# Fourteen scatter-add streams, clearing in 1.6 KB packets and a reordered update stage in a graph network kernel

## The chip, the cores and the metric

One core of a Trainium2 chip runs the whole program once. The metric is the device time of that run in microseconds (us). The times of the kernel before are 3835.6, 3843.22 and 3844.84 us; the median is 3843.22 us.

## What is computed

The input is a graph of 3,125 nodes and 50,000 edges, sorted by destination (`dst`), with 128 numbers a node. Four graph networks follow one another, each with a residual sum and a layer norm behind it:

```python
for l in range(2):                       # first network, a typed graph transformer
    k, q, v = (typed_linear(h, ntype, W) for W in (Wk[l], Wq[l], Wv[l]))
    kT, vT = k x Watt[l, head, etype], v x Wmsg[l, head, etype]   # for all 32 edge types
    att = edge_softmax((kT[src, etype] * q[dst]).sum() * pri / sqrt(16), dst)
    hag = segment_sum(vT[src, etype] * att, dst)
    h = silu(typed_linear(hag, ntype, Wa[l])) * alpha + h * (1 - alpha)
    h = (h - mean) * rsqrt(var + 1e-5) * g + b
# second network: sums over neighbours; third: radial network silu(silu(e8 @ A1 + b1) @ A2 + b2) @ A3
# on 8 edge features; fourth: two graph convolutions with batch norm
```

The second and the fourth network sum over neighbours by a product with a dense matrix of 3,200 x 3,200 counts (how many edges lead from node to node).

## The kernel before, in words

**Stages.** Each stage is a block of its own: all engines meet at its end. In order: `prepare` (indices), then for each of the two layers `project` (`qkv`), `relation_table` (`tab`), `attention` (`att`) and `update` (`upd`); then the other networks, where `adjacency` reads the count matrix three times.

**The count matrix** lies in HBM. Each of its rows has 3,200 cells and 8 more (`AW = NP + STREAMS`), one for the end of each stream. It is cleared by 25 DMAs of 1604 KB each (`wipe_matrix`, L433 to L436), which write a node's row of 12.8 KB as one packet; six of them are issued in `prepare`, nineteen in `project` of layer 0, on SP's queue, behind 16 small loads of marks (`load_chunks`). `query_rows`, 25.7 MB, is cleared in `prepare` in the same way by 16 DMAs (L240). `K.wiped` and `K.cleared` count them; only POOL waits for them, at the start of `tab0` (L1499).

**Scatter-adds.** The 50,176 edges are 392 tiles of 128. For each tile POOL issues one indirect DMA that adds 128 numbers to 128 cells (L1465), after `search` on VectorE has merged the repeats in a tile. The tiles form 8 streams of 49 consecutive tiles, and two tiles of one stream may meet in a cell; so the add number i of a stream waits until number i-1 has landed (`added[k]`). A turn is one tile of each stream. Fixed numbers of turns lie in the stages (`COUNTS`), in tiles: 112 in each `tab`, 24 in each `att`, 48 in each `upd`, 24 in `qkv1`. The search goes by units of the same eight tiles.

**`relation_table`.** TensorE makes keys and values for all 32 types, VectorE and ScalarE copy them from PSUM, SP stores them in 100 DMAs of 1 MB (L1524). Meanwhile POOL scatters 25 tiles of query rows (L1501), issues four gathers (L1506), and then its scatter-adds; a last direct DMA (L1511) and the wait for all landings end the stage on POOL.

**`update`.** n = 10 rounds of four slots. POOL gathers a round's attention sums (four DMAs, L718), from the third round on with four scatter-adds behind them, and issues the rest at the end. VectorE scales (`scale`), TensorE transposes (`flip`), ScalarE copies (`turn`), TensorE multiplies by the typed weight (L761), ScalarE applies silu (L815), VectorE blends with h and takes mean and variance (`blend`), ScalarE takes the root (L797), VectorE the reciprocal (`finish`), ScalarE normalises (L789), VectorE applies gain and shift (`grade`). Between a round's transposes and its typed products both engines do the round's radial pairs (two or three of 24 or 25 in all): two matmuls with 512 columns (L732, L739), two silus (L772, L779) and a store on ScalarE's queue (L781).

## Time and profile before

| what | value |
|---|---|
| time of the profiled execution | 3847.27 us |
| its span | 3845.6 us |
| median of three runs | 3843.22 us |
| busy: TensorE, VectorE, ScalarE, POOL | 68%, 47%, 29%, 57% of the span |
| mean granted TensorE clock | 0.776 of full speed |
| DMA, mean | 227 GB/s |
| the 392 scatter-adds (L1465) | 620.0 us busy, 1.58 us each, 255.1 us idle before them, of which 185.9 us behind the landing of an earlier one |
| `prepare` and `qkv0`, then `tab0` | to 306 us, to 625 us |
| `att0`, `upd0`, `qkv1`, `tab1` | to 1205, 1361, 1465, 1783 us |
| `att1`, `upd1` | to 2368, 2528 us |

"Busy" is the time in which an engine executes; an issue of an indirect DMA counts as work of POOL. Idle time is put down to what ended it. The page's chain of waits covers only the last microseconds of the program, so the stages have to be read one by one.

### The profile page before, as it was taken

The page shows a single profiled execution, that of the slowest core. Times are in us where ns is not written, and L with a number is a line of the kernel's source. Part 1 is how long each engine was busy: PE and PEld are TensorE (multiplying, and loading weights), DVE is VectorE, ACT ScalarE, POOL GpSimd, SP SyncE. Part 2 cuts the span into 40 slices and gives each one's busy share as a digit, 9 for nine tenths or more (in the row PEclk, how much of TensorE's full clock was granted, in tenths as well). Part 3 has the DMA queues.
Part 4 walks back from the last instruction along what each step waited for, and adds up shares of the span by engine and source line. Part 5 has one row for each costly group of instructions (what it writes and reads, how often), then busy time and mean ns, then how long its engine had stood idle before and what let it go on. Part 6 is the DMA issues. An engine that isn't in the chain of part 4 may idle for free. (4 is left out here: it accounts for less than half of the span.)

```text
span 3845.6 us, 42073 instructions
## 1 busy us (share of the span) xinstructions
PE 2610.9 (68%) x11696; PEld 1711.6 (45%) x11696; DVE 1813.0 (47%) x4239; ACT 1122.4 (29%) x2928; POOL 2202.2 (57%) x1985
## 2 busy tenths in 40 slices
PE   1537992666662658992666663638968888859696
PEld 1325662555551335662555552334444444434343
DVE  6524442555562455442555552431058888830303
ACT  0113440222221743440222222730034555510001
POOL 4316557777777876557777777860047777720000
PEclk9966555888876875555788786868969999969797
DMA  9988996898975448996898884447546666547372
GB/s 350 310 339 320 395 391 155 259 266 263 268 224 109 73 120 306 396 391 169 255 263 261 267 235 94 92 133 235 194 117 192 188 187 190 153 169 271 123 272 85
DMA packets 656434, 872.83 MB, mean 227 GB/s; under 512 B 120594, under 2 KB 540761, under 8 KB 615653
## 3 DMA queue, kind: packets, MB, share of 16 engines
q1 hardware_dynamic: 298564, 567.61, 42.0%
q0 software_dynamic: 120320, 158.13, 18.0%
q10 hardware_dynamic: 237360, 144.89, 12.3%
q8 instruction: 79, 1.29, 0.1%
q14 instruction: 111, 0.90, 0.1%
HBM read 441.21 MB, written 429.28 MB: 226 GB/s over the span
## 5 line engine op out<-in xcount | busy, mean ns | idle before, releaser
L1698 POOL DMA_INDIRECT att_rows<-table,kvrow x784 | 797.4, 1017 | 247.6 <-issue 232.8
L1465 POOL DMA_INDIRECT matrix<-count,place x392 | 620.0, 1582 | 255.1 <-DMA matrix<-count,place 185.9
L2101 POOL DMA_INDIRECT msg_rows<-rows,msg_src x392 | 404.0, 1031 | 338.1 <-DMA msg_src<-in_src_pt 218.9
L1756 PE MATMUL att_po<-att_message,att_mate 128*128 128x264 f32 (+1 forms) x1568 | 394.5, 407 | 10.8 <-ACT att_out L1824 5.4
L1548 DVE COPY tab_part<-tab_bank 128x512 f32<-128x512 f32 x400 | 257.5, 686 | 294.4 <-DMA table<-tab_part 276.3
L1589 PE MATMUL tab_bank<-wk,tab_kv 32*128 32x256 f32 x1600 | 363.9, 696 | 30.5 <-DVE tab_part L1548 19.2
L1725 PE MATMUL att_pq<-a,att_mate 128*128 128x128 f32 x1152 | 215.2, 347 | 223.3 <-DVE att_prod L1882 222.8
L1756 PEld LDWEIGHTS att_po<-att_message,att_mate 128*128 128x128 f32 x1568 | 305.9, 238 | 65.2 <-DVE att_message L1933 26.2
L1882 DVE TENSOR_TENSOR att_prod<-att_rows,att_pq 128x512 f32<-128x512 f32 x196 | 134.8, 688 | 424.0 <-DMA att_rows<-table,kvrow 423.6
L1589 PE MATMUL tab_bank<-wv,tab_kv 32*128 32x256 f32 x1600 | 332.2, 618 | 0.0
L1573 ACT ACTIVATE tab_part<-tab_bank 128x512 f32<-128x512 f32 x400 | 221.7, 594 | 312.8 <-DMA table<-tab_part 297.8
L1725 PEld LDWEIGHTS att_pq<-a,att_mate 128*128 128x128 f32 x1152 | 194.5, 252 | 252.8 <-issue 249.0
L1409 PE MATMUL gsum_acc<-gsum_cells,h_rows 128*128 128x512 f32 (+1 forms) x700 | 287.6, 563 | 17.0 <-DMA gsum_cells<-matrix 17.0
L1824 ACT ACTIVATE att_out<-att_po 128x136 f32<-128x136 f32 (+1 forms) x784 | 224.6, 336 | 243.4 <-PE att_po L1756 236.4
L1589 PEld LDWEIGHTS tab_bank<-wk,tab_kv 32*128 32x128 f32 x1600 | 204.4, 302 | 179.6 <-DVE tab_part L1548 149.1
L1589 PEld LDWEIGHTS tab_bank<-wv,tab_kv 32*128 32x128 f32 x1600 | 234.6, 321 | 12.4
L1725 PE MATMUL att_pq<-att_query,att_mate 128*128 128x128 f32 x416 | 78.8, 350 | 195.4 <-DMA att_query<-query_rows 103.6
L1409 PEld LDWEIGHTS gsum_acc<-gsum_cells,h_rows 128*128 128x128 f32 x700 | 131.2, 193 | 174.7 <-issue 157.2
L2155 ACT ACTIVATE msg_sc<-msg_rows,msg_edge 128x128 f32<-128x128 f32 x392 | 125.3, 390 | 264.9 <-DMA msg_rows<-rows,msg_src 261.5
L2139 PE MATMUL msg_pm<-msg_prod,down 128*128 128x512 f32 x392 | 189.4, 607 | 3.0 <-DVE msg_total L2228 1.4
L1874 DVE TENSOR_TENSOR att_mate<-att_rank,rank_own 128x512 f32<-128x512 uint8 x196 | 134.3, 685 | 97.7 <-DMA att_rank<-rank 97.7
L2112 PE MATMUL msg_pu<-ident,msg_sc 128*128 128x128 f32 x784 | 110.7, 284 | 102.3 <-ACT msg_un L2163 88.1
(403 smaller groups left out, 4147.2 us busy)
## 6 DMA issues: line engine op xcount, KB each, us to landing
table<-tab_part SPq DMA_DIRECT2D x200, 1024.0 KB
gsum_cells<-matrix SPq DMA_DIRECT2D x50, 1604.0 KB
att_sums<-att_out ACTq DMA_DIRECT2D x196, 272.0 KB
matrix<-a SPq DMA_DIRECT2D x25, 1604.0 KB
nb_cells<-matrix SPq DMA_DIRECT2D x25, 1604.0 KB
a<-query_rows SPq DMA_DIRECT2D x144, 256.0 KB
query_rows<-a SPq DMA_DIRECT2D x16, 1568.0 KB
att_message<-in_ea_rows SPq DMA_DIRECT2D x98, 256.0 KB, 4.6
```

Source lines behind the costliest of these rows:

```text
L1409: nc.tensor.matmul(acc[c][:, 0:m], rows[:, i, :], cells[i % R][:, part(c)], start=i == 0, stop=False)
L1465: nc.gpsimd.indirect_dma_start(D.matrix, bass.IndirectOffsetOnAxis(ap=K.place[:, col:col + 1], axis=0), K.count[:, col:col + 1], None, com ...
L1548: nc.vector.tensor_copy(quad_columns(c // 2, c % 2), bank[c // 2 % 2 * 4 + c % 2][:, :].rearrange("p (n r d) -> p n r d", n=2, d=QUAD)).th ...
L1573: nc.scalar.activation(quad_columns(c // 2, 2 + c % 2), bank[c // 2 % 2 * 4 + 2 + c % 2][:, :].rearrange("p (n r d) -> p n r d", n=2, d=QUAD),
L1589: last = nc.tensor.matmul(bank[q % 2 * 4 + quad][:, k * (W // 2):(k + 1) * (W // 2)], kv[u][rows, k, :], w[rows, q * 8:q * 8 + 8, :].rearr ...
L1698: nc.gpsimd.indirect_dma_start(rows[g % RR][:, j, :], None, D.table, bass.IndirectOffsetOnAxis(ap=K.kvrow[:, t:t + 1], axis=0)).then_inc(r ...
L1725: last = nc.tensor.matmul(pq[g % 2][:, j * P:(j + 1) * P], mate[g % RS][:, j, :], query[g % RQ][:, j, :], start=True, stop=True)
L1756: nc.tensor.matmul(po[j][:, 0:w], mate[h % RS][:, j, :], message[h % RM][:, j, 0:w], start=True, stop=True).then_inc(summed, 1)
L1824: nc.scalar.activation(out[k][:, j, 0:w], po[j][:, 0:w], ACT.Copy).then_inc(copied, 1)
L1882: nc.vector.tensor_tensor(prod[g % 2][:, :, :], rows[g % RR][:, :, 0:P], pq[g % 2][:, :].rearrange("p (j d) -> p j d", j=J), ALU.mult).the ...
L2101: nc.gpsimd.indirect_dma_start(rows[g % RR][:, j, :], None, D.rows, bass.IndirectOffsetOnAxis(ap=src[:, t:t + 1], axis=0)).then_inc(rows_i ...
L2139: nc.tensor.matmul(pm[n][:, :], down[n][:, :], prod[n][:, :], start=True, stop=True).then_inc(mapped, 1)
```

## The change

Three things are changed.

1. **Streams.** 14 streams of 28 tiles in place of 8 of 49. The adds are placed tile by tile (`count_part`) and no longer by whole turns: 140 in each `tab`, 24 in each `att`, 24 in each `upd`, 16 in `qkv1`. The search keeps its units of eight (`SEEK`). A matrix row grows from 3,208 to 3,216 cells.
2. **Clearing.** Both clearings write packets of 1.6 KB (1,568 B and 1,608 B) from one zero strip in place of 12.5 and 12.8 KB. Three wipes are in `prepare`, 22 in `project`, now ahead of the marks' loads.
3. **Update.** The roots, reciprocals and means of five rounds are taken at once, twice a stage; a round's typed products stand ahead of its radial pairs, and the transposes of round k+1 ahead of the products of round k, on TensorE and on ScalarE; the hidden rows are stored by SP in place of ScalarE; the next layer's weights are loaded behind the radial network's; POOL adds five tiles a round in rounds 4 to 8, and none in the first four.

```diff
-STREAMS = 8
+STREAMS = 14
...
+COUNTS = {"qkv0": range(0), "tab0": range(0, 140), "att0": range(140, 164), "upd0": range(164, 188),
+          "qkv1": range(188, 204), "tab1": range(204, 344), "att1": range(344, 368), "upd1": range(368, TILES)}
+UPDATE_TILES = 5
+AW = NP + 16
+STRIP = AW // 8
...
-EARLY_WIPES = 6
+EARLY_WIPES = 3
...
-                sp.dma_start(rows[:, i * WIPE:(i + 1) * WIPE], K.zero[:, 0:WIPE]).then_inc(K.cleared, 16)
+                sp.dma_start(rows[:, i * WIPE:(i + 1) * WIPE].rearrange("p (b c) -> p b c", b=8),
+                             K.zero[:, 0:WIPE // 8].unsqueeze(1).broadcast_to([P, 8, WIPE // 8])).then_inc(K.cleared, 16)
...
-        sp.dma_start(cells[i], K.zero[:, 0:AW]).then_inc(K.wiped, 16)
+        sp.dma_start(cells[i].rearrange("p (b c) -> p b c", c=STRIP),
+                     K.zero[:, 0:STRIP].unsqueeze(1).broadcast_to([P, AW // STRIP, STRIP])).then_inc(K.wiped, 16)
...
+def count_part(nc, K, D, pool, cols, added, begin, end):
+
+    for i in range(begin, min(end, len(cols))):
+        k = cols[i] % STREAMS
+        if i >= STREAMS:
+            pool.wait_ge(added[k], i // STREAMS * 16)
+        nc.gpsimd.indirect_dma_start(D.matrix, bass.IndirectOffsetOnAxis(ap=K.place[:, cols[i]:cols[i] + 1], axis=0),
+                                     K.count[:, cols[i]:cols[i] + 1], None, compute_op=ALU.add).then_inc(added[k], 16)
```

The update's orders, TensorE and ScalarE, and VectorE below:

```diff
+            flip_in(0)
+            for k in range(n):
+                kinds = [nc.tensor.value_load(K.tile_type[0:1, k * J + j:k * J + j + 1], min_val=0, max_val=NTYPES - 1)
+                         for j in range(J)]
+                if k + 1 < n:
+                    flip_in(k + 1)
...
+                pe.wait_ge(copied, k + 1)
...
+                last.then_inc(mapped, 1)
...
+            turn_out(0)
+            for k in range(n):
+                if k + 1 < n:
+                    turn_out(k + 1)
+                act.wait_ge(mapped, k + 1)
...
+                for i in radial_pairs(k):
+                    first_layer(i)
+                    if i >= 1:
+                        second_layer(i - 1)
+                if k == HALF:
+                    root(0)
+                if k > HALF:
+                    normalise(k - HALF - 1)
+            second_layer(many - 1)
+            root(1)
+            for k in range(HALF - 1, n):
+                normalise(k)
...
+            scale(0)
+            scale(1)
+            for k in range(n):
+                if k == HALF + 1:
+                    finish(0)
+                blend(k)
+                if k + 2 < n:
+                    scale(k + 2)
+                if k >= HALF + 2:
+                    grade(k - HALF - 2)
+            grade(HALF - 2)
+            finish(1)
+            for k in range(HALF - 1, n):
+                grade(k)
```

## Rows read from the trace of the kernel before

**Rows 1.** Busy by stretch, first layer: stretch, length, engines with counts, clock, DMA share, GB/s.

```profile
180.00:260.00 80.00, 33.94 (x118) 17.81 (x118) 23.39 (x160) 12.54 (x28) 0.00 (x0) 0.74 1.02 419
...
260.00:300.00 40.00, 17.74 (x96) 15.71 (x97) 17.54 (x127) 6.95 (x12) 23.80 (x25) 0.67 0.49 141
...
330.00:580.00 250.00, 240.73 (x1446) 164.40 (x1440) 117.44 (x183) 107.57 (x227) 153.37 (x103) 0.51 1.07 392
...
580.00:620.00 40.00, 0.00 (x0) 0.00 (x0) 2.05 (x3) 0.93 (x2) 31.57 (x22) 0.50 0.35 59
```

**Rows 2.** Timeline of POOL, first table stage: start, length, what ended the wait.

```profile
306.89 1.03 POOL L1501 DMA_INDIRECT query_rows<-qkv_rows,start  x1 [11.34 <-issue]
...
344.26 1.63 POOL L1465 DMA_INDIRECT matrix<-count,place  x1 [0.30 <-issue]
...
355.51 1.55 POOL L1465 DMA_INDIRECT matrix<-count,place  x1 [0.31 <-issue]
...
370.64 1.55 POOL L1465 DMA_INDIRECT matrix<-count,place  x1 [0.56 <-DMA matrix<-count,place]
...
591.03 1.55 POOL L1465 DMA_INDIRECT matrix<-count,place  x1 [0.30 <-issue]
...
618.90 1.55 POOL L1465 DMA_INDIRECT matrix<-count,place  x1 [0.30 <-issue]
```

**Rows 3.** DMA issues between 430 and 560 us.

```profile
table<-tab_part SPq DMA_DIRECT2D x49, 1024.0 KB
...
matrix<-count,place POOLq DMA_INDIRECT x49
```

**Rows 4.** DMA queues between 1510 and 1520 us, second table stage: packets, MB, share.

```profile
q1 hardware_dynamic: 535, 3.86, 97.4%
...
q0 software_dynamic: 723, 0.00, 11.2%
```

**Rows 5.** Timeline of POOL, end of the second table stage.

```profile
1749.49 1.55 POOL L1465 DMA_INDIRECT matrix<-count,place  x1 [0.30 <-DMA matrix<-count,place]
...
1777.36 1.55 POOL L1465 DMA_INDIRECT matrix<-count,place  x1 [0.30 <-issue]
```

**Rows 6.** DMA queues between 185 and 255 us (clearing).

```profile
q1 hardware_dynamic: 2250, 25.61, 86.4%
...
q10 hardware_dynamic: 2588, 3.85, 14.7%
```

**Rows 7.** DMA queue of ACT between 1378 and 1422 us (no clearing).

```profile
q10 hardware_dynamic: 4228, 6.30, 41.0%
```

**Rows 8.** First projection: a store of ACT, and the first row gather of POOL.

```profile
192.15 10.06 ACTq L615 DMA_DIRECT2D qkv<-qkv_out  x1
...
264.44 1.06 POOL L556 DMA_INDIRECT qkv_rows<-qkv,slot  x1 [93.36 <-DMA qkv<-qkv_out]
```

**Rows 9.** Update stages: POOL, then the last work of DVE, of both layers.

```profile
1206.16 0.99 POOL L718 DMA_INDIRECT upd_got<-att_sums,end_slot  x1 [9.29 <-POOLq L73]
...
1311.51 0.94 POOL L718 DMA_INDIRECT upd_got<-att_sums,end_slot  x1 [0.30 <-issue]
...
1359.75 0.69 DVE L890 TENSOR_TENSOR hx<-upd_norm,upd_shift 128x512 f32<-128x512 f32 x1
...
2369.07 1.01 POOL L718 DMA_INDIRECT upd_got<-att_sums,end_slot  x1 [9.61 <-POOLq L73]
...
2511.62 0.69 DVE L890 TENSOR_TENSOR hx<-upd_norm,upd_shift 128x512 f32<-128x512 f32 x1
```

**Rows 10.** Groups of ACT in the first update.

```profile
L797 ACT ACT_TABLE_LOAD x10 | 12.8, 1283 | 0.2
...
L772 ACT ACT_TABLE_LOAD x9 | 11.5, 1283 | 15.8 <-PE upd_ph L732 15.7
```

**Rows 11.** Second projection: last store of ACT, first row gather of POOL.

```profile
1406.09 0.37 ACTq L615 DMA_DIRECT2D qkv<-qkv_out  x1
...
1423.27 1.04 POOL L556 DMA_INDIRECT qkv_rows<-qkv,slot  x1 [0.30 <-issue]
```

More of the change, by code:

```diff
@@ L335, in _ @@
             pe.wait_ge(celled, 1)
-            for i in range(EARLY_TURNS):
+            for i in range(EARLY_UNITS):
                 lay_cells(nc, K, pe, S, i, i)
@@ L704, in _ @@
                 sp.dma_start(bb[h, 1:2], D.L2_gnn_b2.rearrange("(p o) -> p o", o=1)).then_inc(net_in, 16)
+            if next_w is not None:
+                load_projection(nc, K, D, sp, l + 1, next_w)
+            for i in range(many):
+                v = pairs.start + i
+                sp.wait_ge(lit2, i + 1)
+                sp.dma_start(D.hidden[:, v * W:(v + 1) * W], h2[i % 4][:, :]).then_inc(hid_out[i % 4], 16)
             if store:
                 for k in range(n):
-                    sp.wait_ge(done, k + 1)
+                    sp.wait_ge(graded, k + 1)
                     sp.dma_start(out[k], hx[:, part(k), 0:P]).then_inc(stored, 16)
                 sp.wait_ge(stored, 16 * n)
+            for u in range(4):
+                sp.wait_ge(hid_out[u], 16 * len(range(u, many, 4)))
         @block.gpsimd
         def _(pool):
-            half = STREAMS // 2
             for k in range(n):
@@ L739, in second_layer, with flip_in @@
                 nc.tensor.matmul(ph2[i % R][:, :], a2[:, :], h1[i % R][:, :], start=True, stop=True).then_inc(hid2, 1)
-            pe.wait_ge(loaded, 48)
-            for k in range(n):
+            def flip_in(k):
                 pe.wait_ge(scaled, k + 1)
@@ L747, in _ @@
                 last.then_inc(turned, 1)
+            flip_in(0)
[4 more added lines that the diff above has]
+                    flip_in(k + 1)
+                if k == 0:
+                    pe.wait_ge(loaded, 48)
+                pe.wait_ge(copied, k + 1)
+                if k >= 2:
+                    pe.wait_ge(lit, k - 1)
+                for j in range(J):
+                    last = nc.tensor.matmul(acc[k % 2][:, j * P:(j + 1) * P], turn[k % 2][:, j * P:(j + 1) * P],
+                                            w[:, bass.ds(kinds[j], 1), :].rearrange("p t o -> p (t o)"), start=True, stop=True)
+                last.then_inc(mapped, 1)
                 if k == 0:
@@ L774, in second_layer @@
             def second_layer(i):
-                v = pairs.start + i
                 act.wait_ge(hid2, i + 1)
@@ L1512, in _ @@
             pool.wait_ge(opened, 16 * J + 16)
[L1513 to L1514 removed]
+            counted_all(pool, cols, added)
         @block.sync
```

211 lines of the change are left out of this document (77 added, 134 removed).

## The prediction

> **What bounds the kernel now.** No engine is busy all the time, and the stages meet at barriers, so I read stage by stage what ends each. First the busy time by stretch [rows 1]. From 180 to 260 us the DMA engines are full (419 GB/s) and no engine works much: the first projection waits behind the clearing. From 260 to 300 they are half idle. From 330 to 580 they are full again (392 GB/s): the table is being stored. From 580 to 620 every engine but POOL has finished: POOL issues scatter-adds alone. Then POOL's timeline in that stage [rows 2]: the adds begin at 344.3 us, 37.4 us behind the first scatter; up to the fifteenth at 370.6 none waits for a landing, then each waits; from 591.0 on none does, and the last sixteen follow at 1.86 us. The second table stage ends alike [rows 5]. Both update stages end with VectorE's last shift, 154 and 143 us behind the first gather [rows 9]; the second projection is held by POOL, which comes to its row gathers at 1423.3 us, while ScalarE's last store is issued at 1406.1 [rows 11].
>
> **What limits an add while the table is stored.** With eight streams at most eight are under way. The add issued at 355.5 (the seventh) frees the one at 370.6: it took 15 us from its issue, and nothing had waited before. In the steady part 49 adds and 49 stores are issued in the same 130 us [rows 3], one of each in 2.65 to 2.7 us; so a landing takes about 8 x 2.7 = 21.6 us. If an add needed a fixed 21.6 us, the ninth, issued 15 us behind the first, would have waited; it didn't. The time grows with the adds in front, and add and store go one for one: I read it as a queue served at one packet of adds for one 8 KB packet of the table. More adds in flight then lengthen the queue, not its rate. Against this stands one row: while the queue fills, the adds' queue moves 723 packets beside 535 of the table in 10 us [rows 4], more than one for one on the mean of the engines. A landing needs all sixteen, so the slowest would have to be the one at one for one.
>
> **Step 1, clearing.** The same 66.8 MB (16 x 1568 KB and 25 x 1604 KB) are written. Long packets cost 0.864 x 16 x 70 us for 25.61 MB, 26.5 bytes a ns and engine, 423 GB/s on sixteen [rows 6]; packets of 1.5 KB cost 23.4 [rows 6] and 21.8 [rows 7], 350 to 374 GB/s. The new ones have 1.6 KB: I take 360 GB/s, bounds 350 and 423. In `prepare` 30.6 MB at 360 take 85 us as 35.5 MB at 423 take 84; its end comes some 5 us earlier (150 for 155), because its small transfers no longer stand behind 12.8 KB packets. In `project` ScalarE's issue of a store of 768 KB took 10 us [rows 8]: one 1.5 KB packet for one of 12.8 KB. It will flow, and the gathers, which came at 264.4, start near 206. But this gives nothing by itself: POOL's scatters in `tab0` wait for the wipes. I sum the DMA work from 152 us on: 22 wipes are 36.1 MB, 100 us; ten stores 22; 25 gathers of 196 KB 12; small loads 5. The wipes have landed at 291 in place of before 306.9, when POOL began [rows 2]. The projection is over by then (near 250), so the half idle stretch is used up; of some 40 us idle, 27 are paid back to the smaller packets.
>
> The Trainium skill (DMA: Bandwidth & Descriptors, Specifications) holds that a transfer of 512 B or more runs at line rate. The rows differ (21.8 and 23.4 against 26.5); by the page the clearing would cost nothing more. That is the third rival.
>
> **Step 2, `tab0`.** First add at 291 + 37.4 = 328. Table stores took from 310 to 589 us; with four buffers ready they need 272, to 563. An add lands 10 us behind the first issue, then one in 2.7 us; issued by then are the landed ones and those in flight. The sum gives (589 - 344 - 10)/2.7 + 1 + 8 = 96 for before, and 96 were issued. After: (563 - 328 - 10)/2.7 + 1 + 14 = 98. The other 42 of 140 follow at 1.86 us: the last starts at 641, before at 618.9. **+22 us.** The depth of 14 is worth six adds here; if it gave none, the stage would be 11 us longer.
>
> **Step 3, `tab1`.** Nothing ahead of it moves inside the stage. 28 adds more, six of them taken by the depth, 22 x 1.86. **+41 us**, bounds +30 (twelve taken) and +52 (none).
>
> **Step 4, `att`.** 24 adds in both. Nothing.
>
> **Step 5, `qkv1`.** 16 adds in place of 24: 8 x 1.87 = 15 us, until the last store (1406.1 + 4 to land) is late next, at 1410 for 1423.3. **-13 us.**
>
> **Step 6, updates.** ScalarE loses 17 of some 20 table switches of 1.28 us [rows 10] and the issue of 24 stores, which SP takes on behind its loads; a wait for the fifth pair's buffer is covered by four buffers. VectorE loses 16 small instructions. That alone would make a round some 8 us instead of 12. But POOL now paces: rounds 4 to 8 need 4 x 1.26 + 5 x 1.88 = 14.4 us each. The last round's gathers ended 107 us behind the first [rows 9] with 28 adds ahead of them, and have 24 now: 99 us. Behind them: landing 2.5, scale 1.3, transposes 1.1, products of round 8 1.5 (they now stand behind the transposes of round 9), two pairs 3.4, four register loads 1.9, products 1.5, silu 0.6, three pairs and the last layer 5.8, switch and root 1.6, reciprocals 0.4, six normalisations 9.9, the last grade 1.4: 33 us, together 132. Before 154: **-22 us**. In layer 1, 143 and 130: **-13 us**. The weights of the next layer are loaded later; the next stage needs them 100 us on, which covers them. If the rounds were free of POOL both would gain some 12 us more; if the new order costs what it saves, nothing. Bounds 0 and -60 for both.
>
> **Sum.** +22 + 41 - 13 - 22 - 13 = **+15 us**. The profiled execution took 3847.27, 4 us over the median of 3843.22; so 3862 on its own scale and **3858 us** against the median.
>
> **The rivals.**
> - *The queue was short, not full.* Fourteen in flight lift the rate of the adds to POOL's own 1.86 us. For it: rows 4. Against it: equal counts over 130 us and the growing landing time. Then 140 adds take 260 us, `tab0` ends its adds at 588 (-31), `tab1` at 1503 + 260 = 1763 (-12): -31 - 12 - 48 = -91, **3752 us**. It decides from a pace below 2.58 us: four more adds served in each table stage are worth the 15 us. The Trainium skill (DMA: Bandwidth & Descriptors, Queues, rings and completion order) has an engine drain a packet of some 9 to 17 descriptors before it switches. If the adds went in such packets, a long queue would be served several for one; rows 3 show one.
> - *Packets of 1.6 KB cost no more.* The wipes land 20 us earlier, at 271: -5, **3838 us**. Against it rows 6 and 7, both of stores of the same kind.
> - *The update gains nothing.* Transposes of the next round hold products, and with them the silu and the pairs, behind POOL's gathers; if a round is served in series, the 35 us are lost: **3893 us**. Against it: TensorE has some 7 us of work in a 14 us round.
> - *The change doesn't do what it says:* two roots a stage and fourteen semaphores are plain in the code; nothing to doubt.
>
> **Chances.** Forecast 0.47; its own range, by the price of clearing (-10, +5), the depth (+-11 a stage) and the updates (+-15), is 3835 to 3885. Rivals 0.18, 0.17 and 0.10; 0.08 is left for the updates gaining twice as much or a stage I did not see. A measurement of this kernel tells 0.3% (11.5 us) from no change: 3832 to 3855 is the same. The forecast gives slower 0.35, same 0.10, faster 0.02; the first rival faster 0.18; the second same 0.10, faster 0.05, slower 0.02; the third slower 0.09 and same 0.01; the rest adds 0.03 each to faster and same, 0.02 to slower. Faster 0.28, same 0.24, slower 0.48. The range has to reach into the first rival's side: a partly faster queue lies between 3752 and 3858. 3765 to 3890 leaves out half of that rival and little above.
>
> **What would show it.** Right: in the table stages adds at 2.7 us with a landing of 38 us, as many adds as stores; a tail of some 42 and 38 adds behind the last store; the wipes' end near 291 us; clearing at 350 to 374 GB/s; POOL idle ahead of the first scatter; updates of 130 us with three or four switches. Wrong: adds at 1.9 us beside full stores, no tail; clearing at over 400 GB/s; an update that ends over 140 or under 120 us behind its first gather.

## The result, and the profile after

**The kernel after takes 3897.97 us (median of four runs, 3887.02 to 3908.33), the kernel before 3844.03; the ratio is 1.0145, 95% interval 1.0130 to 1.0161.** It is slower, as forecast, but by 54 us in place of 15, and 8 us beyond the end of the range. The profiled execution has a span of 3894.7 us.

A table of the stages comes out of both timelines: a stage ends where the first instruction of the next one begins.

| stage | before, us | after, us | difference | predicted |
|---|---|---|---|---|
| everything up to the end of `tab0` | 625.2 | 680.7 | +55.5 | +22 |
| `att0` | 580.2 | 580.5 | +0.3 | 0 |
| `upd0` | 156.1 | 134.2 | -21.9 | -22 |
| `qkv1` | 103.4 | 91.0 | -12.4 | -13 |
| `tab1` | 318.8 | 362.7 | +43.9 | +41 |
| `att1` | 584.6 | 587.1 | +2.5 | 0 |
| `upd1` | 159.4 | 136.1 | -23.3 | -13 |
| all behind it | 1317.9 | 1322.5 | +4.6 | 0 |

So the first line carries nearly all of the error. Busy by stretch of the kernel after (columns as in [rows 1]):

```profile
180.00:260.00 80.00, 42.20 (x199) 26.06 (x199) 36.82 (x257) 21.43 (x42) 20.93 (x22) 0.84 1.05 348
260.00:300.00 40.00, 8.97 (x48) 7.44 (x46) 12.34 (x88) 2.95 (x7) 2.83 (x3) 0.59 1.06 312
280.00:300.00 20.00, 0.00 (x0) 0.00 (x0) 0.00 (x0) 0.00 (x0) 0.00 (x0) 0.50 1.07 300
330.00:580.00 250.00, 243.63 (x1453) 167.11 (x1456) 116.49 (x182) 107.14 (x228) 164.96 (x114) 0.50 1.07 391
600.00:672.00 72.00, 0.00 (x0) 0.00 (x0) 0.00 (x0) 0.00 (x0) 59.63 (x39) 0.50 0.23 1
```

Between 260 and 300 us the DMA engines were half idle before [rows 1]; now they are full, yet they move only 312 GB/s, and from 280 to 300, at 300 GB/s, no compute engine does anything. The projection's work is over (ScalarE's last piece is at 273 us), and the stage isn't. SyncE's timeline says why:

```profile
117.43 179.54 SPq L441 DMA_DIRECT2D matrix<-a  x25
297.02 5.21 SPq L448 DMA_DIRECT2D chunk_bias<-start_bias  x1
...
316.89 0.37 SPq L1531 DMA_DIRECT2D query_nodes<-qkv_rows  x1
```

The issues of the 25 wipes are stretched over 179.5 us, the last small load of marks stands behind them, and only then does SyncE come to the barrier. POOL's timeline shows what follows:

```profile
317.74 1.03 POOL L1515 DMA_INDIRECT query_rows<-qkv_rows,start  x1 [54.02 <-issue]
...
355.10 1.63 POOL L1477 DMA_INDIRECT matrix<-count,place  x1 [0.30 <-issue]
...
412.80 1.55 POOL L1477 DMA_INDIRECT matrix<-count,place  x1 [0.30 <-issue]
414.84 1.55 POOL L1477 DMA_INDIRECT matrix<-count,place  x1 [0.49 <-DMA matrix<-count,place]
```

```profile
602.64 1.55 POOL L1477 DMA_INDIRECT matrix<-count,place  x1 [0.30 <-issue]
...
671.39 1.55 POOL L1477 DMA_INDIRECT matrix<-count,place  x1 [0.30 <-issue]
```

The first scatter-add comes at 355.1 us, where 328 was forecast. 32 adds go out before one waits for a landing (14 did before [rows 2]); then the pace is the old one. The DMA issues between 430 and 560 us, the stretch of [rows 3]:

```profile
table<-tab_part SPq DMA_DIRECT2D x49, 1024.0 KB
matrix<-count,place POOLq DMA_INDIRECT x49
```

49 and 49 again: with fourteen in flight an add comes round in 14 x 2.69 = 37.6 us, with eight it was 8 x 2.69 = 21.5. From 602.6 on the adds go alone, the last 38 of them at 1.86 us. The second table stage ends in the same way (compare [rows 5]):

```profile
1839.68 1.57 POOL L1477 DMA_INDIRECT matrix<-count,place  x1 [0.30 <-issue]
...
1849.75 1.05 POOL L1711 DMA_INDIRECT att_rows<-table,kvrow  x1 [7.61 <-POOLq L77]
```

The updates, POOL's last gather and VectorE's last shift in layer 0, then the same in layer 1 (compare [rows 9]; first gathers at 1261.90 and 2436.81):

```profile
1357.94 0.94 POOL L729 DMA_INDIRECT upd_got<-att_sums,end_slot  x1 [0.30 <-issue]
```

```profile
1393.59 0.69 DVE L899 TENSOR_TENSOR hx<-upd_norm,upd_shift 128x512 f32<-128x512 f32 x1
```

```profile
2567.49 0.69 DVE L899 TENSOR_TENSOR hx<-upd_norm,upd_shift 128x512 f32<-128x512 f32 x1
```

The shifts end 132.4 and 131.4 us behind the first gathers; 132 and 130 had been forecast. ScalarE's table loads in the first update fell from some 20 [rows 10] to four:

```profile
L824 ACT ACT_TABLE_LOAD x2 | 2.6, 1283 | 0.0
L815 ACT ACT_TABLE_LOAD x2 | 2.6, 1283 | 0.0
```

And in the second projection ScalarE's last store and POOL's first row gather stand close together, where POOL was 17 us late before [rows 11]:

```profile
1439.66 0.37 ACTq L619 DMA_DIRECT2D qkv<-qkv_out  x1
```

```profile
1444.26 1.03 POOL L562 DMA_INDIRECT qkv_rows<-qkv,slot  x1 [2.78 <-issue]
```

### The profile page after: what moved, and what is told of

Read it like the earlier page. It is cut to its first block and busy times, and to the rows that moved or that the text cites. A ratio compares the mean times of both kernels' runs of the same rounds, so it can differ in the third digit from the quotient of the medians.

```text
span 3894.7 us, 41929 instructions
## 1 busy us (share of the span) xinstructions
PE 2595.7 (67%) x11696; PEld 1700.8 (44%) x11696; DVE 1808.1 (46%) x4207; ACT 1082.4 (28%) x2880; POOL 2204.4 (57%) x1985
## 5 line engine op out<-in xcount | busy, mean ns | idle before, releaser
L1561 DVE COPY tab_part<-tab_bank 128x512 f32<-128x512 f32 x400 | 257.2, 685 | 335.0 <-DMA table<-tab_part 265.1
L1602 PEld LDWEIGHTS tab_bank<-wv,tab_kv 32*128 32x128 f32 x1600 | 235.4, 322 | 12.4
L1737 PEld LDWEIGHTS att_pq<-att_query,att_mate 128*128 128x128 f32 x416 | 71.4, 257 | 299.5 <-DVE att_mate L1886 193.2
```

Of the source, the lines that this page charges most:

```text
L1561: nc.vector.tensor_copy(quad_columns(c // 2, c % 2), bank[c // 2 % 2 * 4 + c % 2][:, :].rearrange("p (n r d) -> p n r d", n=2, d=QUAD)).th ...
L1602: last = nc.tensor.matmul(bank[q % 2 * 4 + quad][:, k * (W // 2):(k + 1) * (W // 2)], kv[u][rows, k, :], w[rows, q * 8:q * 8 + 8, :].rearr ...
L1737: last = nc.tensor.matmul(pq[g % 2][:, j * P:(j + 1) * P], mate[g % RS][:, j, :], query[g % RQ][:, j, :], start=True, stop=True)
```

## The experiments

Sixteen runs in four batches, each batch on one chip with the kernel before beside it. These chips are slower than the first one: the kernel before took 4219.7, 4261.8, 4229.37 and 4276.32 us there. Most of the difference is in `att` (663 to 695 us for 580 to 587) and in the messages. Table and update stages of the kernel after are within 4 us of its first trace; there is no trace of the kernel before on these chips. Stage lengths are compared within a batch, and whole times as ratios to the kernel before of the same batch. Diffs are against the kernel after.

### First batch: which part of the clearing, whether packets set the adds' pace, the update alone

**Long packets, in the new order.** In both clearings:

```diff
-  sp.dma_start(rows[...].rearrange("p (b c) -> p b c", b=8), K.zero[:, 0:WIPE // 8]...broadcast_to(...))
+  sp.dma_start(rows[:, i * WIPE:(i + 1) * WIPE], K.zero[:, 0:WIPE]).then_inc(K.cleared, 16)
-  sp.dma_start(cells[i].rearrange(...), K.zero[:, 0:STRIP]...broadcast_to(...))
+  sp.dma_start(cells[i], K.zero[:, 0:AW]).then_inc(K.wiped, 16)
```

> The kernel after with one thing undone: both clearings write packets of 12.5 and 12.9 KB again; the order (three wipes early, marks' loads behind the wipes), the 14 streams, the placement and the update stay. After it is: wipes landed at 312 us, SP's issues of them held until 297, the small loads behind them until 315, first table work at 317, first scatter-add at 355, table stage over at 681, whole 3898 us. Theory 'short packets are slow and hold SP': 22 wipes of 1.65 MB at the 376 GB/s that SP's queue had with long packets are 96 us, landed near 256; SP is done near 235; the projection then ends by ScalarE's stores and POOL's gathers, between 295 and 310; first add 333 to 348; 7 to 20 us come back, 3878 to 3891 us. Rival 'the order holds it' (the small loads behind the wipes, whatever the packets): the projection still ends near 317, no change within 4 us, 3894 to 3902. Rival 'ScalarE's stores wait behind long packets and three more wipes': gathers later than 275, projection over behind 315, not faster, 3898 to 3910.

Measured: ratio 1.0087 (1.0049 to 1.0125). POOL's first row gather and first scatter:

```profile
268.76 1.06 POOL L560 DMA_INDIRECT qkv_rows<-qkv,slot  x1 [100.70 <-DMA qkv<-qkv_out]
...
321.57 1.03 POOL L1513 DMA_INDIRECT query_rows<-qkv_rows,start  x1 [21.68 <-issue]
```

The wipes landed at 256.7 us as expected, and SyncE was done at 267. But ScalarE's stores now wait between long packets (gathers at 269, not 233), the gathers' data and the search behind them end at 320.7. In this batch the kernel with short packets and the marks behind them (the half stores below) had its first scatter at 316.6. The second rival came nearest: the projection ended behind 315, though the gathers came at 269 and not behind 275. Long packets hold ScalarE's stores, short ones hold SyncE.

**Marks ahead of the wipes**, packets short:

```diff
-                wipe_matrix(nc, K, D, sp, range(EARLY_WIPES, NT))
                 load_chunks(nc, K, D, sp)
+                wipe_matrix(nc, K, D, sp, range(EARLY_WIPES, NT))
```

> The kernel after with the sixteen small loads of marks ahead of the 22 wipes again; the packets stay at 1.6 KB. Theory 'short packets are slow and hold SP': the wipes land no earlier than 312 us (ten us of issues stand in front of them, so up to 320), SP is held to 298 to 308, the first scatter comes at 312 to 321 for 317.7; table stores may start up to 15 us earlier, the adds not; table stage 0 to 6 us shorter, 3892 to 3898 us. Rival 'the loads behind the wipes are the loss': the projection ends 18 us earlier and so does everything behind it, 3880 us.

Measured: ratio 1.0104 (1.0069 to 1.0140). The stage ended at 307.2 us, and POOL then stood at its wait for the wipes:

```profile
321.68 1.03 POOL L1515 DMA_INDIRECT query_rows<-qkv_rows,start  x1 [64.01 <-DMA matrix<-a]
```

So the small loads behind the wipes held the barrier, but the landing of the wipes, at 320.8, came right behind. The first scatter came 5 us later than in the short-packet kernel of this batch with the marks behind (316.6), whose wipes had landed 9 us earlier: the order of the marks is not the loss.

**Half stores.** A table store of 1 MB becomes two of 512 KB, with packets of 4 KB:

```diff
-                    sp.dma_start(table[..., q * 8:q * 8 + 8, :]..., part[q][:, :, :]).then_inc(stored[q], 16)
+                    for e in range(0, 8, 4):
+                        sp.dma_start(table[..., q * 8 + e:q * 8 + e + 4, :]..., part[q][:, e:e + 4, :]).then_inc(stored[q], 16)
```

> The kernel after with every table store of 1 MB cut in two of 512 KB, so that its packets have 4 KB in place of 8; nothing else. In the steady part of the table stages one add takes 2.7 us, as one store of 1 MB does. Theory 'the queues are served one packet for one': two packets of adds then go in the time of one 8 KB packet, 1.35 us an add, and POOL's own pace of 1.86 us sets it; 140 adds take 260 us, the first table stage ends its adds near 616 in place of 671, the second near 1785 less what went before, if stores keep their rate; 3786 us, and at least 3800 if the stores lose a tenth. Rival 'an add has its own fixed rate beside full stores' (bytes or time, not packets): pace stays at 2.7 us, 3898 us. Rival 'smaller packets cost the stores more than the adds win': stores take over 300 us in place of 272 and end behind the adds, 3830 to 3860 us.

Measured: ratio 0.9915 (0.9890 to 0.9941). DMA issues between 430 and 560 us, and the adds' group on POOL, first of the kernel after, then of this one:

```profile
table<-tab_part SPq DMA_DIRECT2D x92, 512.0 KB
matrix<-count,place POOLq DMA_INDIRECT x71
```

```profile
L1477 POOL DMA_INDIRECT matrix<-count,place x392 | 619.1, 1579 | 233.7 <-DMA matrix<-count,place 157.1 <-issue 76.5
```

```profile
L1477 POOL DMA_INDIRECT matrix<-count,place x392 | 618.1, 1577 | 119.5 <-issue 119.5
```

71 adds in 130 us in place of 49 (53 in the copy of the kernel after of the next batch, where the first 45 adds go out without a wait), and of the 157 us that POOL waited for landings nothing is left. The table stages last 328.6 and 327.5 us; unchanged kernels on these chips have 364 to 367. What had set the pace was the stores of 1 MB beside the adds. The gain is 36 us a stage and not the 56 of the theory, since the stores, 200 of them until 635 us, now end the stage; each took more (315 us for all, 301 with 8 KB packets on these chips). The theory of one for one and the second rival, by which smaller packets cost the stores more, are both in it, one behind the other. Both the size and the number of the stores were changed here; what tells packets from stores stands below, beside the limit of an add.

**The new update alone**, everything else as before, the clearing too (the matrix row stays at 3,216 cells):

```diff
-STREAMS = 14
+STREAMS = 8
-COUNTS = {... "tab0": range(0, 140), "att0": range(140, 164), "upd0": range(164, 188), ...}
+COUNTS = {... "tab0": range(0, 112), "att0": range(112, 136), "upd0": range(136, 184), ...}
-                if 4 <= k < n - 1:
-                    count_part(..., (k - 4) * UPDATE_TILES, (k - 3) * UPDATE_TILES)
+                if k >= 2:
+                    count_part(..., (k - 2) * UPDATE_TILES, (k - 1) * UPDATE_TILES)
...
```

> The kernel before with the new update alone: 8 streams, long packets, six early wipes, marks ahead, the adds placed as before in tiles (112, 24, 48, 24, 112, 24, 48), in the update four adds a round from the third on and sixteen behind the last gather as before. Theory 'POOL paces the new update, VectorE's end follows its last gather by 33 us': the last gather comes 107 us behind the first with the old adds, so the first update ends its grades 140 us behind its first gather (before 154, after 132) and gives 14 us; in the second, POOL's own adds end the stage at 2520 as before, so it gives 0 to 3 us; 3844 - 15 = 3829 us. Rival 'the new order gives all of it': both stages at 130 us, 22 and 23 us, 3799 us. Rival 'the gain came from taking 24 adds out of each update, not from the order': no change, 3844 us.

Measured: ratio 1.0038 (1.0004 to 1.0072). First update, last add of POOL and last shift of VectorE (first gather at 1324.49):

```profile
1466.28 1.55 POOL L1475 DMA_INDIRECT matrix<-count,place  x1 [0.31 <-issue]
```

```profile
1462.01 0.69 DVE L897 TENSOR_TENSOR hx<-upd_norm,upd_shift 128x512 f32<-128x512 f32 x1
```

VectorE ended 138 us behind the first gather (140 expected, 154 before). POOL's last add was issued at 142 us, as in the kernel before (1206.2 to 1348.6), and the stage lasts 153.2 us for 156.1, the second 158.7 for 159.4. POOL ended it: its wait for the last landing was over at 1469.4, and its DRAIN, the first instruction of the barrier, lasted 6.4 us more. In the kernel before that DRAIN was over at 1358.2, only 2.2 us ahead of the end of VectorE's last shift, so an earlier VectorE had little to give. **The new order gives 3 us by itself; its other 19 come only with 24 adds fewer in the stage. These adds, and four a layer from the second projection, are the 28 more in each table stage.** That this run is even slower than before by 0.4% isn't explained by its stages; there is no trace of the kernel before on that chip.

### Second batch: the clearing in full, the placement

**The kernel after, unchanged** (no diff).

> The kernel after, unchanged, as the measure for the runs beside it, since the four runs before this were made on a chip on which the kernel before took 4220 us and the attention stages some 90 us longer than in the first traces. If the chip is like that one, its first table stage should start its scatter at 317 us, end at 685 and its second last 364 us; the time is then 1.009 to 1.012 times the kernel before. If it is like the first chip: scatter at 317.7, ends 681 and 363 long, 1.0145 times.

Measured: 1.0129 (1.0082 to 1.0175), first scatter at 331.6 us, table stages 366.6 and 365.6 us. The wipes landed at 326.0 us, 14 later than on the first chip; with this clearing they landed at 311.8 to 312.2 in each of the other batches, and at 323.7 in the run with the placement as before; the two late ones are on the same chip.

**Clearing undone**: the first two diffs of the first batch together, and

```diff
-EARLY_WIPES = 3
+EARLY_WIPES = 6
```

> The kernel after with the whole clearing as before: packets of 12.5 and 12.9 KB, six early wipes, marks ahead of the other nineteen. Streams, placement and update stay. Theory 'short packets took 56 us longer to land and hold SP' on a chip on which the gathers land as in the first traces: wipes landed at 256, gathers 264 to 295, POOL's first scatter at 307 for 318; 11 us faster than the kernel after, all in the first table stage's end. Rival 'the clearing costs nothing here': where the gathers land late (the runs on the other chip: first scatter at 317.0 with long packets and 316.6 with short ones) the projection's end is set by them, and the time is that of the kernel after within 4 us. Rival 'long packets in the same order' (321.6 there): slower by 5 us.

Measured: 1.0098 (1.0070 to 1.0127). First scatter of the kernel after, then of this one:

```profile
331.63 1.03 POOL L1515 DMA_INDIRECT query_rows<-qkv_rows,start  x1 [72.10 <-issue]
```

```profile
320.57 1.03 POOL L1513 DMA_INDIRECT query_rows<-qkv_rows,start  x1 [22.97 <-issue]
```

11.1 us earlier, and the end of the stage 11.3 us earlier: what the change of the clearing costs in whole on this chip and, by the traces of before and after (306.9 and 317.7), on the first. It isn't a fixed price. On the chip of the first batch the kernel with the old clearing (the update alone) had its first scatter at 317.0 and the one with the new clearing at 316.6; on that of the third batch they came at 318.8 and 317.8. There the old clearing itself ends as late as the new one.

**Placement as before**, 14 streams and the clearing of after: the diff of the update alone without its first two lines.

> The kernel after with the adds placed as before: 112 in each table stage for 140, 48 in each update for 24 (four a round from the third on, sixteen behind the last gather, and in the second 48), 24 in the second projection for 16; 14 streams, short packets and the new update stay. Theory 'an add in a table stage costs 1.86 us behind the last store, one in an update is partly covered': 28 adds less are 52 us less in each table stage (-104); the updates end with POOL's last add again, 153 and 159 us long for 134 and 136 (+42), the projection +12; together -50 us against the kernel after, which is the time of before within 10 us. Rival 'an add costs POOL 1.86 us wherever it stands': no change against the kernel after.

Measured: 1.0018 (0.9993 to 1.0044), in medians 48.6 us less than the kernel after. Table stages 46.6 and 46.9 shorter (the stores end them now, the last at 635.0 us, behind the last add at 630.3), updates 20.6 and 21.2 longer, the projection 14.7. So 28 adds were worth 47 us in a table stage, 24 were worth 21 in an update and 8 were worth 15 in the projection. The placement is the main loss of the change: 48.6 of the 62 us by which the two medians of this batch differ.

**Half stores and clearing undone**: both diffs.

> The kernel after with table stores of 512 KB (packets of 4 KB) and the whole clearing as before; placement of after, new update. Theory 'one packet for one': in the run with half stores alone no add waited for a landing and a table stage lasted 328 us for 364; together with the clearing undone this gives 72 us less than the kernel after, and 11 more on a chip on which the clearing costs that; against the kernel before 0.985 to 0.99. Rival 'stores bound it now': in that run the last store was issued behind the last add (635 for 613 us), so an earlier add gives nothing and the clearing must move the stores themselves: the table's first store starts only with the stage, at 306 to 316 as the projection ends. Then no more than the 72 us come, 0.991.

Measured: 0.9916 (0.9887 to 0.9945). Table stages 330.0 and 329.0 us; last add, then the first gather of the next stage:

```profile
614.89 1.55 POOL L1475 DMA_INDIRECT matrix<-count,place  x1 [0.30 <-issue]
...
648.75 1.06 POOL L1710 DMA_INDIRECT att_rows<-table,kvrow  x1 [31.42 <-POOLq L77]
```

The last store is issued at 638.9. 92 us less than the kernel after in medians, of which 13 are the clearing and 2 x 37 the stores; the rest is in stages that the edit doesn't touch.

### Third batch: packets of middle length, eight streams, a freer update, the 64-byte edge

**Middle strips**, on half stores, with six early wipes and the marks ahead; packets of 4,288 and 3,136 B:

```diff
-STRIP = AW // 8
+STRIP = AW // 3
-  ....rearrange("p (b c) -> p b c", b=8), K.zero[:, 0:WIPE // 8]...
+  ....rearrange("p (b c) -> p b c", b=4), K.zero[:, 0:WIPE // 4]...
```

> The run with half stores and the whole clearing as before, but the clearing in packets of middle length: 3.1 KB for the query rows, 4.3 KB for the matrix (a third of its row), six early wipes, marks ahead. In the runs on the other chips long packets landed the last wipe at 256 us with the row gathers at 264 to 296, short ones at 312 to 326 with the gathers at 229 to 259; POOL's first scatter came at 317 to 321 with long packets. Theory 'only the shortest packets are slow': 4 KB packets of other queues go at 24 to 25 bytes a ns and engine, so the wipes land at 262 to 275, ScalarE's stores pass between them and the gathers start 10 to 25 us earlier, the projection ends at 292 to 308; 10 to 25 us less than with long packets. Rival 'any cut of the packets costs': wipes behind 290 us, no gain or a loss against long packets.

Measured: 0.9893 (0.9834 to 0.9952). First row gather, first scatter:

```profile
244.02 1.06 POOL L562 DMA_INDIRECT qkv_rows<-qkv,slot  x1 [70.37 <-DMA qkv<-qkv_out]
...
298.21 1.03 POOL L1515 DMA_INDIRECT query_rows<-qkv_rows,start  x1 [23.09 <-issue]
```

The wipes landed at 282.3 us (262 to 275 expected), the gathers started 22 us earlier and the first scatter 20.6 us earlier than in the long-packet kernel of this batch (266.1 and 318.8). Neither SyncE nor ScalarE is held long. The whole time doesn't show these 20 us: the medians of this batch are 4186.5 us here, 4190.9 with long packets (with the freer update, below) and 4170.8 with short packets and eight streams, and the intervals overlap. Between the traces of this batch `att0` alone differs by up to 19 us and the messages by 40, in code that is the same.

**Eight streams**, on half stores:

```diff
-STREAMS = 14
+STREAMS = 8
```

> The kernel after with half stores and 8 streams for 14; clearing, placement and update as after. With 14 streams and half stores no add waited for a landing (0.9915 of before, table stages 328 us). Theory 'one packet for one, 8 in flight are enough': eight adds land in 8 x 1.35 = 11 us while POOL needs 15 us to come round, so hardly one waits, the pace stays at 1.86 us and the time within 5 us of that run; fourteen streams are then not needed once the packets are short. Rival 'a landing has a long part that does not shrink with the packets': adds wait, a pace over 2 us, the last of 140 behind the last store, 10 us or more a stage.

Measured: 0.9835 (0.9779 to 0.9891); table stages 327.9 and 327.2 us, to a microsecond those of fourteen streams. The adds' group on POOL:

```profile
L1477 POOL DMA_INDIRECT matrix<-count,place x392 | 617.2, 1575 | 119.5 <-issue 119.5
```

No add waited for a landing. Beside stores of 1 MB six more streams bought six adds a stage; beside stores of 512 KB they buy nothing.

**Twelve adds from each update into the table stage**, on the fourth kernel of the second batch:

```diff
-COUNTS = {... "tab0": range(0, 140), "att0": range(140, 164), "upd0": range(164, 188), ...}
-UPDATE_TILES = 5
+COUNTS = {... "tab0": range(0, 152), "att0": range(152, 176), "upd0": range(176, 188), ...}
+UPDATE_TILES = 2
```

> Half stores, clearing as before, new update, 14 streams, and twelve adds moved from each update into the table stage ahead of it: 152 for 140 there, 12 for 24 in the update (two a round). In the run without this move the last add of a table stage was issued at 614.9 us and the last store at 639, so 12 x 1.86 = 22 us of adds find room beside the stores. Theory 'POOL paces the update': its last gather comes 12 x 1.87 = 22 us earlier, but by then the chain of a round (TensorE, ScalarE, VectorE) is late next; 8 to 15 us less in each update, table stages the same within 4 us; 16 to 30 us in all, 0.985 of before. Rival 'adds beside the stores slow the stores': table stages 5 to 10 us longer. Rival 'the update is bound by its own chain already': nothing gained.

Measured: 0.9911 (0.9880 to 0.9941), no gain over that one (0.9916, another chip). The updates became 128.6 and 127.7 us (133.9 and 136.0 there), the table stages 333.3 and 335.0 (330.0 and 329.0). Last add and first gather of the next stage:

```profile
637.31 1.56 POOL L1475 DMA_INDIRECT matrix<-count,place  x1 [0.30 <-issue]
...
651.97 1.06 POOL L1710 DMA_INDIRECT att_rows<-table,kvrow  x1 [12.22 <-POOLq L77]
```

The last add now comes beside the last store (636.4), and the adds slow the stores a little: 14 us gained, 9 given back. The 12 us that a free update was to give were 5 to 8. POOL's last gather came 22 and 25 us earlier (74 and 71 us behind the first, for 96), VectorE's last shift only 5 and 8: the update's own chain is next.

**Aligned packets**, on half stores; 1,664 B in place of 1,608:

```diff
-AW = NP + 16
+AW = NP + 128
```

> The kernel after with half stores and a matrix row of 3,328 cells in place of 3,216, so that the short packets of the clearing have 1,664 bytes in place of 1,608 and begin at multiples of 64 bytes; 3.5% more bytes in the clearing (the later reads of the matrix grow as much, so the whole time says nothing here). In the traces the short packets to the query rows took 70 ns each, the ones to the matrix 75 beside ScalarE's queue and 91 to 97 when alone. Theory 'packets that begin off a 64-byte edge are slow': 70 to 75 ns a packet all along, the last wipe lands 20 to 35 us earlier than in the run beside it with the same clearing. Rival 'it is the place (all engines write into one block of 1.6 MB) or the count of packets': 90 ns or more between 280 and 300 us, the wipes land as late or up to 5 us later.

Measured: the last wipe landed at 298.2 us, 312.2 in the eight-stream kernel of the same batch with the old row; first scatter 305.5 and 317.8. The pair in the next batch repeats it.

### Fourth batch: the version to keep, and the edge once more

**The kernel with middle strips again**, no new edit.

> The run with middle strips once more, in five rounds, as the version to beat both kernels: half stores, clearing in packets of 3.1 and 4.3 KB with six early wipes and marks ahead; 14 streams, placement and update as after. Its stages: first scatter at 298, table stages 328 us each; 0.985 to 0.992 of the kernel before, against 1.0145 (first chip) and 1.013 (third chip) of the kernel after.

Measured: 0.9863 (0.9837 to 0.9889), first scatter at 300.7, table stages 329.4 and 328.1 us.

**Every second store cut**, on the kernel with middle strips:

```diff
-                    for e in range(0, 8, 4):
+                    size = 4 if q % 2 else 8
+                    for e in range(0, 8, size):
```

> The same with only every second table store cut in two, so that four MB of the table leave in six packets a partition in place of eight. Stores of 8 KB packets took 301 us for the 100, cut ones 315, on chips like these. Theory 'one packet for one': six adds are served in the 12.1 us of four MB, 2.0 us an add; 140 adds end near 274 us behind the first, beside the last store; the stores get back half of the 14 us, so each table stage is 4 to 8 us shorter than with all cut, 318 to 325 us; 0.983 to 0.990. Rival 'an add has a rate of its own that the stores' packets only let through': pace 1.86 as before, the stage ends with the stores all the same. Rival 'the 14 us are the adds' own traffic, not the packets': stage lengths stay at 328 us.

Measured: **0.9828 (0.9797 to 0.9858)**, table stages 325.7 and 325.4 us, 3.7 and 2.7 less than with all cut. Adds went at 1.86 us with no wait (0.3 us in all). That doesn't tell the first two theories apart: served at 2.0 to 2.1 us and issued at 1.86, 140 adds fall some ten to fifteen behind, about what fourteen streams hold. This is the version to keep: faster than both kernels, the kernel before by 1.7%. Against the one with all stores cut the intervals overlap, and only the stage lengths speak for it; the kernel with eight streams and short packets (0.9835) did as well on its chip.

**The kernel after with the aligned row** (the diff of the third batch, 8 KB stores), **beside its unchanged copy.**

> The kernel after with only the matrix row grown to 3,328 cells (clearing packets of 1,664 bytes that begin at multiples of 64), beside an unchanged copy on the same chip. The pair with half stores gave a last wipe at 298 us for 312 and a first scatter at 306 for 318. Theory 'the alignment is half of the late start': here too 12 to 15 us between the two; the rest of the difference to the 291 us of the prediction is the rate of the packets that are aligned (72 to 78 ns for 1,664 bytes, 21 to 23 bytes a ns), so 296 to 300 us. Rival 'that difference was the run, not the edge': both within 4 us. The later reads of the matrix are 3.5% longer, so the whole time says nothing here.

> The kernel after, unchanged, on the same chip as the three beside it: last wipe at 312 to 326 us, first scatter at 317 to 332, first table stage 364 to 367 us long.

Measured: last wipe at 297.5 and 311.8 us, first scatter at 304.8 and 317.1. SyncE's DMA queue between 280 and 295 us (packets, MB, share), aligned, then not:

```profile
q1 hardware_dynamic: 3378, 4.97, 97.9%
```

```profile
q1 hardware_dynamic: 2738, 4.33, 106.3%
```

4.97 MB in 0.979 x 16 x 15 us are 21.2 bytes a ns and engine; 4.33 MB in 1.063 x 16 x 15 are 17.0. A share over 100% means that records overlap; by the clock the two move 331 and 289 GB/s. The difference of 14 us was forecast (12 to 15). Since the row's length sets both where packets begin and how far apart rows lie, the pair doesn't tell these two apart.

## Why the prediction was right and wrong

**Wrong: step 1, clearing, the price of a packet of 1.6 KB.** The range had been 350 to 423 GB/s, taken from packets of 1.5 KB. In the kernel after SyncE's queue had this, between 185 and 225 us and between 280 and 295:

```profile
q1 hardware_dynamic: 5683, 8.99, 67.0%
```

```profile
q1 hardware_dynamic: 2808, 4.44, 106.9%
```

8.99 MB in 0.670 x 16 x 40 us are 21.0 bytes a ns and engine, a little under the lower bound (350 / 16 = 21.9); 4.44 MB in 1.069 x 16 x 15 are 17.3 (by the clock 296 GB/s), far below it. The wipes landed at 312 us, not 291, and the gathers started at 233, not 206. The sum used one price for the whole clearing, and bounded it by packets of 1,536 B, which all begin at a multiple of 64 bytes; those of 1,608 B begin at multiples of 8. The pair with the longer row puts 14 of the 21 us there, or on the stride that changed with it; the other 7 are what packets of 1,664 B take themselves (they land at 298). Then SyncE, held by its own queue, had its small loads to issue behind the last wipe, and the barrier came 5 us behind the landing. The sum had no term for SyncE's issues at all: it put the hold at nothing, with small loads of 5 us as traffic only. So the first add was 27 us late (355 for 328), the stores as well, and with them the last add (671 for 641).

The rival in which packets of 1.6 KB cost no more is wrong as well. The Trainium skill (DMA: Bandwidth & Descriptors, Specifications) has a rule of 512 B, by which the clearing should have cost nothing more; the measurement decides against it here: 26.5 bytes a ns and engine for 12.8 KB [rows 6], 21.2 for 1,664 B, 17.0 for 1,608 B. Whether the engines take turns packet by packet or in groups, the counts of this case can't tell, since equal groups give equal counts too. The Trainium skill (DMA: Bandwidth & Descriptors, Queues, rings and completion order) has an engine take a packet of some 9 to 17 descriptors from one queue before it switches; 49 adds beside 49 stores neither show nor exclude it. So the prediction's remark that a long queue would be served several for one, and that rows 3 show one, doesn't hold. In the trace of the kernel after, between 460 and 580 us, the adds' packets rather come in groups: 3,171 pairs of them start 6 ns apart, where an arbitrary small distance has some 790. The records don't name the engine, so this is a hint.

**Right: the limit of an add while the table is stored.** Full queue, one add for one store: same pace with 14 in flight, a round of 37 us (38 forecast), 102 adds by the end of the stores (98; six more than before in the same 237 us, as forecast), a tail of 38 (42 and 38). The first rival (a short queue) is out: in every run with 8 KB stores, with eight streams or fourteen and on four chips, adds and stores both came every 2.67 to 2.72 us between 460 and 580 us. Its sum was also 2 us off: 1777.4 to 1763 [rows 5] is -14, not -12. Half stores lifted the adds to POOL's own pace; how fast they would go beside 512 KB stores, one of which goes every 1.40 us, isn't seen, as POOL issues none faster than in 1.86.

In the table stage an add and a store have 128 packets each, so the adds alone don't tell "one packet for one" from "one DMA for one". The clearing does. SyncE's and ScalarE's queues between 185 and 225 us, in the kernel before (12.8 KB beside 1.5 KB packets) and with middle strips (4.3 KB beside 1.5 KB):

```profile
q1 hardware_dynamic: 1310, 14.96, 88.3%
q10 hardware_dynamic: 1312, 1.94, 13.0%
```

```profile
q1 hardware_dynamic: 2784, 11.46, 74.4%
q10 hardware_dynamic: 2789, 4.16, 28.1%
```

The numbers of packets are equal to within 0.2%. The bytes are not, and the DMAs aren't either (by the bytes, 9.1 wipes of 1604 KB beside 2.5 stores of 768 KB in the first, 7.0 beside 5.3 in the second). With 1.6 KB packets they are not equal (5,683 and 3,451): ScalarE's issues, at 0.4 us each, were no longer held there, so its queue need not have been full.

**Right: step 3,** 22 adds of tail more at 1.858 us are 40.9. The 3 us above are new: the stage ends 9.3 us behind the last add for 6.3 before, in both layers, and the same 3 us are in step 2. POOL's waits for landings are over 4.7 us behind the last add in both kernels. What grew is its DRAIN behind them, in the first layer 3.65 us for 0.71. The run with the placement of before and fourteen streams had 1.40, the one with 152 adds in the stage 4.63. So by these runs 0.7 us go with the streams and about 0.08 with each add of the stage; why is open.

**Right: step 5,** and ScalarE's last store, which had been named, was the next late one.

**Right in layer 0, short in layer 1: step 6.** The last gather came 96 us behind the first (99 forecast), the rest took 36 (33). In layer 1 the gain was 23 and not 13, because I read the stage's end from VectorE's last shift [rows 9], while the adds ended it. POOL's last add in the kernel before, and the next stage:

```profile
2509.62 1.60 POOL L1465 DMA_INDIRECT matrix<-count,place  x1 [0.30 <-issue]
2528.45 1.01 POOL L956 DMA_INDIRECT open_h_rows<-h_slots,slot  x1 [17.23 <-POOLq L2310]
```

It was issued at 2509.6; POOL's wait for the landings was over at 2519.5, its DRAIN behind them at 2526.2, and the stage ended at 2527.7, 15 us after the last shift. SyncE had seen its last store land at 2520.4, so it wasn't the stores. The update alone showed how much of the whole step hangs on the adds' number: in layer 0 as well the order by itself moved VectorE's end by 16 us and the stage's by 3, and only with 24 adds fewer did the stage follow VectorE. The sum didn't say so. That layer 0 came out to 0.1 us is luck in part, since two errors of 3 us cancelled. The rival by which the update gains nothing was nearly right for the order alone, and wrong for the change.

The total: 15 forecast, 33.5 more up to the end of `tab0` (30.4 by the late last add, 3 by POOL's DRAIN), 3 in `tab1`, 0.6 in `qkv1`, -10 in `upd1`, 7.4 in the attentions and behind `upd1`, to which the sum had given nothing: 49, as the span grew. The medians differ by 54; these 5 us more are between the executions, whose times differ by up to 21 us in the kernel after.

## What to carry to other kernels

When two queues with work share the DMA engines, count packets, not bytes. The queue with tiny packets moved at the pace at which the other one's packets passed (an add every 2.69 us beside 8 KB packets, every 1.86 beside 4 KB), so shorter packets of the big transfer sped up the small ones, and more of them in flight didn't. Packets can be too short as well: a middle length (3.1 and 4.3 KB here, beginning at multiples of 64 bytes) let two queues flow side by side and brought the next stage 20 us forward, though whole times did not resolve that gain. And before a stage is relieved of work, ask what ends it now, and what ends the stage to which the work goes: 24 adds were worth 21 us in an update, and in a table stage, where they stood alone behind the last store, 28 cost 44 to 47.

## What the runs showed that was not expected

- Packets of 1,608 B into matrix rows of 12,864 B took 93 ns on the mean when alone, packets of 1,664 B into rows of 13,312 B 78 ns (between 280 and 300 us; means of the trace's packets); beside ScalarE's queue, between 180 and 220 us, they took 76 and 77. Packets of 1,568 B to the query rows, which begin at multiples of 32, took 80 on the mean and 71 at the median (between 60 and 110 us, kernel after). Only the row's length was changed, so another effect of the new stride isn't excluded, and why nothing shows beside a second queue stays open.
- The medians of the two kinds when alone lie close together (78 and 76 ns): a part of the shorter packets takes much longer, not all of them.
- SyncE was held by its own issues: 22 long wipes were issued in 64 us and had landed 44 us behind the last issue; 22 short ones (marks ahead) took 137 us to issue and had landed 20 us behind it. What holds the issues isn't shown.
- With cut stores an add's round with eight streams is 8 x 1.86 = 14.9 us, POOL's own, where it was 21.5.
- The same program took 10 to 11% more on four other chips, nearly all of it in stages that gather rows; the table stages were as long as on the first to within 4 us.
